# Attention and the second feed-forward stage in one block, with both feed-forward openings in another order

## The reference, cut to what matters

```python
x = x + 0.5 * ffn(layernorm(x))        # "ffn1"
x = x + attention(layernorm(x))        # "att"
x = x + 0.5 * ffn(layernorm(x))        # "ffn2"

def ffn(x):      # 8 experts of width 256, 2 active for each token
    scores = sigmoid(x @ gate_w.T + balance_bias)
    topk, idx = top_k(scores, 2);  topk /= topk.sum() + 1e-6
    comb = zeros(T, 8) with topk at idx
    h = silu(einsum('td,ehd->teh', x, w1))
    return einsum('te,ted->td', comb, einsum('teh,edh->ted', h, w2))

def attention(x):  # 16 heads of width 8, causal, two softmaxes a1, a2 for each head
    out = (a1 - lam * a2) @ v                   # for each head
    out = out * rsqrt(mean(out * out) + 1e-6) * head_norm_w * 0.8
    return out @ Wo.T + bo
```

## Time and profile before

| What | us |
|---|---|
| median of 3 runs | 1843.06 |
| lowest and highest | 1840.89 and 1844.34 |
| the profiled execution: its time | 1844.34 |
| the profiled execution: span from the first to the last instruction | 1842.6 |
| ffn1: first instruction to the last store issued | 0.3 to 433.8 |
| attention: first instruction to the last store issued | 436.2 to 1405.5 |
| ffn2: first instruction to the end of the span | 1407.3 to 1842.6 |

### The profile page before, as it was taken

How to read it: one execution, slowest core, us unless ns; L and a number is a source line. 1 busy time by engine, 2 the same in 40 slices (tenths; PEclk the granted TensorE clock), 3 DMA queues, 4 the chain that set the end, 5 groups by cost and what they waited for, 6 DMA issues and landing times. The chain is left out here.

```text
span 1842.6 us, 43587 instructions
## 1 busy us (share of the span) xinstructions
PE 1615.4 (88%) x16768; PEld 1235.1 (67%) x16768; DVE 1343.6 (73%) x3034; ACT 1199.4 (65%) x1581; POOL 1319.9 (72%) x836
## 2 busy tenths in 40 slices
PE   4999999995478998988989888998872799999998
PEld 3787778784356666666666666666651688778787
DVE  5777777765678788888878788788732677777775
ACT  4777777772156676666666576676662577777776
POOL 4888888875447677767767677677634688888885
PEclk9999999997589999999999999999996899999999
DMA  3333233332222332332232322332302233233331
GB/s 115 104 116 111 86 104 116 104 104 53 78 67 74 94 89 63 93 92 71 83 88 69 88 83 70 92 87 65 88 17 71 99 115 114 82 105 115 104 110 63
DMA packets 143678, 163.16 MB, mean 89 GB/s; under 512 B 13244, under 2 KB 125582, under 8 KB 142478
## 3 DMA queue, kind: packets, MB, share of 16 engines
q1 hardware_dynamic: 143472, 160.38, 28.5%
HBM read 91.20 MB, written 14.70 MB: 57 GB/s over the span
## 5 line engine op out<-in xcount | busy, mean ns | idle before, releaser
L292 POOL TENSOR_TENSOR ffn_h_low<-ffn_h,ffn_h_high 128x1024 fp32r<-128x1024 f32 x192 | 458.8, 2403 | 94.8 <-ACT ffn_h_high L341 94.8
L1046 ACT ACTIVATE att_prob<-att_ring 128x1024 f32<-128x1024 f32 x384 | 390.3, 1024 | 181.4 <-PE att_ring L1280 180.7
L1159 DVE TENSOR_REDUCE att_nmax<-att_ring 128x4 f32<-128x1024 f32 (+1 forms) x384 | 453.2, 1215 | 39.8 <-PE att_ring L1280 36.8
L479 DVE TENSOR_TENSOR ffn_h<-ffn_up,ffn_comb_wide 128x1024 f32<-128x1024 f32 x256 | 311.1, 1215 | 125.9 <-ACT ffn_up L334 125.7
L334 ACT ACTIVATE ffn_up<-ffn_up 128x1024 f32<-128x1024 f32 x256 | 258.1, 1008 | 201.9 <-PE ffn_up L567 200.2
L341 ACT ACTIVATE ffn_h_high<-ffn_h 128x1024 fp32r<-128x1024 f32 x256 | 269.3, 1052 | 0.7 <-DVE ffn_h L479 0.7
L978 POOL TENSOR_TENSOR att_rrms<-att_ms_eps,att_minus_halves 128x32 f32<-128x32 f32 x32 | 174.1, 5440 | 67.6 <-DVE att_ms_eps L1185 67.6
L1280 PE MATMUL att_ring<-att_qs,att_kd 64*128 64x256 bf16 (+1 forms) x2048 | 153.2, 249 | 76.9 <-DVE att_nmax L1159 24.9
L567 PE MATMUL ffn_up<-ffn_xt_high,ffn_w_high 128*128 128x512 f32 x512 | 214.8, 419 | 1.6 <-DVE ffn_h L479 1.5
L284 POOL TENSOR_TENSOR ffn_ez<-ffn_e_const,ffn_nz 128x16 f32<-128x16 f32 x64 | 185.7, 2903 | 38.8 <-DVE ffn_nz L405 38.8
L580 PE MATMUL ffn_y<-ffn_h_high,ffn_w_high 128*128 128x512 f32 x512 | 205.4, 401 | 6.4 <-POOL ffn_h_low L292 5.0
(11 more groups left out here) (152 smaller groups left out, 3248.8 us busy)
## 6 DMA issues: line engine op xcount, KB each, us to landing
ffn_comb_wide<-ffn_comb_d SPq DMA_DIRECT2D x128, 512.0 KB, 5.7
att_qs<-att_parts SPq DMA_DIRECT2D x192, 128.0 KB, 2.4
att_kd<-att_parts SPq DMA_DIRECT2D x192, 128.0 KB, 2.4
ffn_x<-x SPq DMA_DIRECT2D x32, 256.0 KB, 3.1
ffn_w<-w SPq DMA_DIRECT2D x4, 1024.0 KB, 7.6
x<-ffn_out SPq DMA_DIRECT2D x16, 256.0 KB, 2.4
att_x<-x SPq DMA_DIRECT2D x32, 128.0 KB, 2.3
att_xr<-x SPq DMA_DIRECT2D x32, 128.0 KB, 2.3
```

The lines of the kernel that those rows point to most:

```text
L292: nc.gpsimd.tensor_tensor(hts[1][:, e % NH], h[:, e % NH], hts[0][:, e % NH], ALU.subtract).then_inc(low_by_pool, 1)
L479: nc.vector.tensor_tensor(h[:, e % NH], up[:, e % NUP], comb_wide[:, b.c % NW, e].unsqueeze(1).to_broadcast([P, HE, FT]), ALU.mult).then_i ...
L1046: nc.scalar.activation(prob[:, u % NP], ring[:, ORDER.index((kind, u)) % 3], ACT.Exp, scale=SCALE).then_inc(prob_ready, 1)
L1159: nc.vector.tensor_reduce(nmax[:, b, :, h0:h0 + cnt], ring[:, pos % 3] .rearrange("p (s h k) -> p s h k", s=2, k=width), AX.X, ALU.max, ne ...
```

## The change

1. Attention and ffn2 become one program block. `ffn` no longer opens a block: it returns for each queue a `setup`, a `body` and an `end`. ffn1 runs them as before (`ffn_alone`). For ffn2, each queue of attention runs them behind its own turns. There is no meeting of all queues between the two stages any more.
2. The last attention turn is cut in two. Its first step ("XT", 0) stays where it was; then come ffn2's set-up and the whole of `body(Block(-2))`; then the rest of the last attention turn; then ffn2 from c = -1 on. In SP's queue the residual load of the last sequence stays in the first part and the store of the last sequence is in the second.
3. Semaphores guard the memory that both stages use. Before its set-up each queue waits for six semaphores of attention (`gone`); PE waits for the last reads of OT and OP before the first up product (`banks_free`); each load of x by ffn2 waits until attention has stored the rows (`stored_for`). Tiles that the last turn's rest still uses are allocated apart (`tail`), and ffn2's tiles take the place of the others (`rest.close()`). In PSUM `scratch` moves ahead of `turn_ps` and `gate_ps`.
4. In both feed-forward stages, in the opening c = -1 alone: POOL does both `gate_exp` parts before `ln_rstd`, DVE does `mean_shift` behind gate part 0, and `weight_low(2)` moves from e = 4 to e = 6, behind the last gate round and `xt_low`, and ahead of `logits`.

```diff
-def ffn(nc, tag, x_in, x_out, w):
+def ffn(nc, tag, x_in, x_out, w, ctx, after=None):
...
+    def sync(sp):
         def load_x(b):
+            if after:
+                after.stored(sp, b)
             sp.dma_start(x[:, b.slot()], x_in[b.at(FT):b.at(FT, FT), :].rearrange("(t p) d -> p t d", p=P)
...
+        def setup():
+            if after:
+                after.to_sync(sp)
             load_x(Block(0))
...
     def gpsimd(pool):
...
                 low(*b.behind(e, LOW_LAG))
-                if e == 1 and read.exists():
+                if e == 1 and read.exists() and b.c != -1:
                     ln_rstd(read)
                 if e in (0, 1) and gated.exists():
                     gate_exp(gated, e)
+                if e == 1 and b.c == -1:
+                    ln_rstd(read)
...
     def vector(dve):
...
-                if e == 2 and read.exists():
+                if e == 2 and read.exists() and b.c != -1:
                     mean_shift(read)
                 if e in (2, 3, 4, 5) and gated.exists():
                     gate(gated, 2 * (e - 2))
+                if e == 2 and b.c == -1:
+                    mean_shift(read)
                 if e == 5 and read.exists():
                     xt_low(read)
                 if e == 4 and b.c == -2:
                     weight_low(0)
-                if e == 4 and b.c == -1:
+                if e == 6 and b.c == -1:
                     weight_low(2)
                 if e == 7 and read.exists():
                     logits(read)
...
+        def up_free(b):
+            if after and b.c == 0:
+                after.to_up(pe)
...
+                if e == 0:
+                    up_free(b)
                 up_product(b, e)
...
+WHOLE, OPENING, CLOSING = slice(None), slice(1), slice(1, None)
+
+def turns(body, first, following):
+    setup, ffn_body, end = following
+    for i in range(first, B + 2):
         body(Turn(i))
+    body(Turn(B + 2), OPENING)
+    setup()
+    ffn_body(Block(-2))
+    body(Turn(B + 2), CLOSING)
+    for c in range(-1, FB + 1):
+        ffn_body(Block(c))
+    if end:
+        end()
...
+        def gone(engine):
+            engine.wait_ge(pv_done, 4 * B)
+            engine.wait_ge(prob_ready, 12 * B)
+            engine.wait_ge(pe["T"], 12 * B)
+            engine.wait_ge(o_copied, 4 * B)
+            engine.wait_ge(max_in, 32 * B)
+            engine.wait_ge(left_step, 4 * B)
+
+        def banks_free(engine):
+            engine.wait_ge(read["OT"], B)
+            engine.wait_ge(read["OP"], B)
+
+        def stored_for(engine, b):
+            engine.wait_ge(stored, 16 * min(B, FT // S * (b.c + 1)))
...
                 def body(turn, part=WHOLE):
...
-                    if turn.runs(-3):
+                    if turn.runs(-3) and part is not CLOSING:
                         wait_apart(sp, read["OP"], turn.at(-4, 1, 1))
                         sp.dma_start(xr[:, turn.slot(-3)], x_in[turn.at(-3, S):turn.at(-3, S) + S, :]
...
-                    if turn.runs(-3):
+                    if turn.runs(-3) and part is not OPENING:
                         wait_apart(sp, read["OP"], turn.at(-3, 1, 1))
...
-                turns(body, -1)
-                sp.wait_ge(stored, 16 * B)
+                turns(body, -1, ffn_sync(sp))
...
-    ffn(nc, "ffn1", a["x"], x1, a)
-    attention(nc, "att", x1, x2, a)
-    ffn(nc, "ffn2", x2, out, a)
+    ffn_alone(nc, "ffn1", a["x"], x1, a)
+    attention_and_ffn(nc, "att", x1, x2, "ffn2", out, a)
```

More of the change, by code:

```diff
@@ L93, in blocks @@
         body(Block(c))
-def ffn(nc, tag, x_in, x_out, w):
-    with ExitStack() as ctx:
[L105 to L206, removed]
-            before = sum(p < e for p in POOL_LOW)
-            if e in POOL_LOW:
-                wait(engine, low_by_pool, b.at(len(POOL_LOW), before + 1))
-            else:
-                wait(engine, low_by_dve, b.at(ON_DVE, e - before + 1))
-        weights = ((gate_w, (gate_ws[:, 0], gate_ws[:, 1])), (w1, [t[:] for t in w1s]),
-                   (w2, [t[:] for t in w2s]))
@@ L216, in ffn, with run, ffn_alone @@
+def run(engine, program):
+    setup, body, end = program(engine)
+    setup()
+    blocks(body)
+    if end:
+        end()
+def ffn_alone(nc, tag, x_in, x_out, w):
+    with ExitStack() as ctx:
+        sync, gpsimd, scalar, vector, tensor = ffn(nc, tag, x_in, x_out, w, ctx)
         with nc.Block() as block:
@@ L295, in body @@
-                def body(b):
-                    gated, read = b.shift(1), b.shift(2)
-                    for e in range(E):
-                        low(*b.behind(e, LOW_LAG))
-                        if e == 1 and read.exists():
-                            ln_rstd(read)
-                        if e in (0, 1) and gated.exists():
-                            gate_exp(gated, e)
-                blocks(body)
+                run(pool, gpsimd)
             @block.scalar
             def _(act):
-                def weight_high(n):
-                    nc.scalar.activation(weights[n][1][0], weights[n][0][:], ACT.Copy).then_inc(split_high, 1)
@@ L370, in _ @@
[L370 removed]
+                run(act, scalar)
             @block.vector
             def _(dve):
[L374 to L384 removed]
@@ L528, in _ @@
[L528 removed]
+                run(dve, vector)
             @block.tensor
             def _(pe):
[L532 to L550 removed]
@@ L614, in _ @@
-                blocks(body)
+                run(pe, tensor)
 NSLOT = 3
@@ L1002, in _, with body @@
                 nc.gpsimd.memset(v[:, :, :, :, HD:HD + 1], 1.0).then_inc(v_set, 1)
-                def body(turn):
-                    for kind, u in ORDER:
+                def body(turn, part=WHOLE):
+                    for kind, u in ORDER[part]:
                         for n in range(2):
@@ L1297, in weigh, with body @@
                     last.then_inc(pv_done, 1)
-                def body(turn):
-                    for pos, (kind, u) in enumerate(ORDER):
+                def body(turn, part=WHOLE):
+                    for pos, (kind, u) in tuple(enumerate(ORDER))[part]:
                         buf = ring[:, pos % 3]
```

806 lines of the change are left out of this document (471 added, 335 removed).

## The result

The changed kernel takes 1824.01 us (median of 4 runs, 1822.12 to 1824.34), against 1843.7 for the kernel before beside it (4 runs, 1840.89 to 1845.09). The ratio is 0.989, with a 95% interval of 0.9865 to 0.9915: 19.7 us less between the medians, where the prediction had 15.2.

A forecast was written before the change was run, and what follows sets the result against it. It took the hole with PE nearly idle between attention and ffn2, and ffn1's same opening, as what the change can shorten. 12.65 in ffn2 plus 2.5 in ffn1 made 15.2 us off the median 1843.06: 1828 us, range 1824 to 1833.5.

The forecast's parts named there:

- The two openings: Starts of ffn1 and ffn2: 2.5 us saved in ffn1 and 12.65 in ffn2, 15.2 in sum.
- SP's and POOL's set-up: Attention to ffn2: first x load 11.57 us earlier, `ln_rstd(0)` ending 10.2 earlier, the first `gate_exp` at 1409.58 instead of 1420.38.
- The seven waits: Semaphore waits before ffn2's set-up, long satisfied: bounded between zero and some 0.5 us, taken as 0.3.
- The closing half of the last turn: ffn2's opening: DVE queued behind the last turn's add, so gate rounds begin 1.4 us later than the powers would allow.
- rival B: ffn2's opening: weights land late, each us delaying the gate rounds one us; 3 us late saves 12.2, 1830.9 us; chance 0.12.
- The order in ffn1: ffn1's opening: new order saves 2.5 us, 0.55 at MAX8 plus 2.0, or 3.1 without the second power's 0.57 loss.
- Rigid blocks: Both feed-forward stages after their openings: steady blocks keep their own period, unchanged at 24.9 us.
- A: ffn2's opening: DVE's subtraction blocks behind the POOL power, 0.95 us less; 14.2 saved, 1828.9 us; chance 0.12.
- C: Both openings: new order worth nothing, as another wait of ACT or PE sets `comb`; 10.7 saved, 1832.4 us; chance 0.10.
- D: Openings: waits cost nothing (0.3), closing half doesn't hold DVE (1.4), ffn1's power loses nothing (0.6); 17.5 saved, 1825.6; chance 0.07.
- E: ffn2 after the hole: TensorE's clock stays at 0.50; a whole block so gives 1852.6 us; chance 0.04.
- F: Whole kernel: the merged program does nothing, 1843 us; chance 0.01.

The follow-up runs named there:

- before_low: Kernel before, with only the last step of attention's row maxima moved from POOL to an earlier step on DVE, so their write goes sooner; 1823.21 us.
- after_low: Changed kernel with the last step of attention's row maxima on DVE at an earlier step, timed beside before_low; 1806.22 us, 17.0 less than before_low.
- before_again: Kernel before, unchanged, run again for a second trace; 1843.53 us, ratio 0.9997 to the kernel before.
- after_again: Changed kernel, unchanged, run again for a second trace and more timings; 1826.53 us, ratio 0.9898 to the kernel before.
- after_low_dve: Changed kernel with the last step of attention's row maxima moved from POOL to an earlier step on DVE; 1808.23 us, ratio 0.9806 to the kernel before.
- w_low_later: Changed kernel with `weight_low(1)` moved to where `weight_low(2)` stood, and `weight_low(2)` behind the statistics of c = 0; 1829.03 us, ratio 0.9918 to the kernel before.
- merge_only: Changed kernel with the old order of both openings: merged block and split last turn, without part 4; 1835.66 us, ratio 0.9959 to the kernel before.
- both: Changed kernel with the edits of after_low_dve and w_low_later together; 1806.31 us, ratio 0.9795 to the kernel before.

## Why the prediction was right, and where it failed

**The two openings: right in place, 1.8 us short.** 17.03 measured in the pair of profiles and 17.0 between the medians of `before_low` and `after_low`, where the sum was 15.2. The 1.8 are 1.2 of hold that didn't come, 0.4 by which the first `gate_exp` starts earlier, and 0.2 in ffn1. That the pair has 17.03 is partly luck: `before` has 44.67 us at the boundary where `before_again` and `before_low` have 44.08 and 44.19, and `after` 30.38 where the other traces with that boundary have 30.36 to 31.39.

- SP's and POOL's set-up: the load goes 0.62 after the power's start (0.76 predicted). The seven waits were taken at 0.3. On POOL they lie under the power and cost nothing, on SP some 0.2. `ln_rstd(0)` ends 7.22 after the power's start, where 7.6 was predicted, and the first `gate_exp` begins at +14.21 (14.59 predicted).
- The closing half of the last turn was the mis-sized term: 1.4 us of hold on the gate rounds was predicted. They began at 1407.17, 0.2 behind the end of the powers (1406.95), and MAX8 began 1.28 behind that end, where before has 0.87 and the prediction 2.5. So the hold is 0.4 in place of 1.6, and MAX8 stands 7.06 behind the first `gate_exp` where 8.3 was the sign given. What failed in it is the landing of the weights. The prediction took one row for what they need, 9.86 us from the first load's issue to use, and that row is the slowest of the 14 traces: its second load took 9.37 us, the others 7.6 to 9.3. Here ACT used them 8.8 after the first issue. Late weights cost what rival B says; they came 1.0 later in `after_again`, and 0.6 later in `after_low_dve`, whose boundary is 31.12.
- The order in ffn1: 2.74 against 2.5. The second power lost its 0.57 under `weight_low(1)`, as taken: 6.35 in place of 5.78, and `w_low_later`, without that subtraction, has 5.77.
- `comb` begins 4.70 after MAX8 in ffn2, as predicted (4.99 in ffn1). `weight_low(2)` was hidden with 0.93 to spare (0.75 predicted).
- Rigid blocks: the steady block has 24.73 of 24.90 us, and ez1 to the end is 402.9 and 403.1.

**The rivals.** A fell: `weight_low(1)` starts 3.8 us into the two powers (1404.97) and takes 2.28, as ever. The other direction holds: in after, `after_again` and `merge_only` `ln_rstd(1)` ends 0.87 behind the end of `weight_low(1)`, however long it had to wait (1.21, 2.23 and 2.99 long, against 1.0 with nothing beside it). So of what the Trainium skill (SBUF — State Buffer, "Who interferes with whom") says, that the later one of the two waits until the first is done, these traces bear out the half in which POOL is the later one, and not the half in which DVE is. B was met in one trace at 1.0 us and in another at 0.6. C fell: the order is worth 5.0 alone, and 9.8 on top of the merge. D, given 0.07, came nearest in size (17.5 against 17.0): two of its three conditions came true for the most part, the waits and the hold, and the third didn't, since the ffn1 power did lose its 0.57. E fell with the clock rows: the stretch after the hole is at 0.50 for 4 us and at 0.92 in the next. F fell.

**The steps that failed.** The time lies 1.2 us below the range, and it took two misses of the same sign to put it there; the mechanism of both parts was as forecast. The first is the term of the sum above: the hold of the closing half, put at 1.4 and measured at 0.2 to 0.4, because the landing of the weights was taken from one slow row. With the 17.0 that the change is worth, the forecast would have been 1826, and either miss alone would have left the time inside the range. The second is in the numbers: "Without a change, medians of this kernel agree within about 0.2% (3.7 us; the runs spread over 3.4)", and the 1 us of spread set on A to D from it. Three runs were too few to tell. The kernel before lies between 1835.4 and 1850.66 in 26 executions on one chip, and its medians beside other kernels were 1843.7, 1841.57, 1844.44 and 1835.88, the last three on three chips. So a range made of the change's own terms (1824 to 1833.5) was too narrow: of the 19.7 measured 17.0 are the change, and 2.7 lie within a spread that the kernel has without it. In the next set the same two kernels were 15.0 apart. "Both stages should run on rigidly" holds for the feed-forward stages; attention, between them, was not looked at, and its profile had the signs: 13 waits of PE for `att_qs`, 20.2 us in all, and three stretches at a granted clock of 0.50 in its steady part.

**What stays open.** What delays the 48 KB write by up to 2 us, and what puts the instruction packets where they are, was not isolated: the one attempt to move them didn't move them. That each slow write has such a packet beside it is a coincidence in time seen 26 times out of 26 in before and after, not a cause shown. A packet alone is not enough either: in `after_low` three such packets started 1.17 to 1.38 us behind the issue of a write and left it at 1.54 to 1.55. Shown is that the edit with the earlier write takes the long turns away. Which slow writes are followed by a fall of the clock (two to four in each trace) stays open as well. The 2.2 us that the pair of profiles has between ez1 and the first power weren't followed up; the twelve other traces have 520.3 to 522.3 there, with the change or without.

## What to carry to other kernels

When two stages meet, follow every queue past the meeting point and ask what each engine has queued behind the tail of the first; here the merge and the order of the opening were worth 7.2 and 5.0 us alone and 17.0 together, because in the old order the second gate power stands behind `ln_rstd(1)`, which in the merged kernel waits 1.05 us for its statistics and is then held by a subtraction (2.99 us long), and the new order puts that power in front. Before a range is given, look at the stages that the change does not touch: a stage whose equal turns differ in length (26.8 to 31.3 us here) has a spread of its own, and it may hold as much as the change does (13 to 21 us here). A small transfer on which the next step waits should be given some us of slack, above all where an idle PE is followed by a lower clock: issuing it 4 us sooner took 13 us (`after_low_dve` against after) to 21 us (`both` against `w_low_later`) out of attention.

## What was not expected of the hardware

- A DMA write of 48 KB took 1.5 us from issue to landing in 19 turns and 2.0 to 3.7 us in 13, each of these with a 16 KB packet of the instruction queue beside it (before and after).
- In a stage in which PE is busy nine tenths of the time, one idle time of 2.46 us was followed by 6.8 us at a granted clock of 0.50; each of the 24 turns of 29.1 us or more in eight traces has 3.4 or 6.8 us of it, against 26.8 us for a normal turn.
- A POOL power on a tile of 128x4, 1.00 to 1.02 us long, ended 0.87 us after a DVE subtraction of 128x2048 with two inputs under which it began, whether it began 0.34, 1.36 or 2.12 us before that end. The subtraction itself took 2.28 us everywhere, also when it began inside a POOL power.
- Seven waits on semaphores long past their value cost some 0.2 us on SP and six nothing to be seen on POOL, where an instruction of 5.44 us ran meanwhile.
- Of two loads of 1 MB issued in a row the second landed 7.98 us after its issue in one execution and 9.32 in another of the same kernel (7.6 to 9.4 in 14 traces).
